# A two-layer transformer on one core: the loop over iterations 2 to 14 written out, waits on constants

## What is computed

```python
x = layernorm(x + L0_attn(x))      # rmsnorm, q/k/v, softmax(q k / 8) v, output projection, bias
x = layernorm(x + L0_ffn(x))       # shared expert + sum over 8 experts, weighted by the top-2 router gates
x = layernorm(x + L1_attn(x))      # per token: 16 heads of 8, scores between heads of the same token
x = layernorm(x + L1_ffn(x))       # sum over 8 experts, weighted by the top-2 router gates
```

## Time and profile before

| | |
|---|---|
| median of 3 runs | 1562.2 us (1561.91 to 1562.41) |
| the profiled execution | 1567.07 us, span 1565.3 us |
| TensorE matmul / weight load, busy | 1421.9 us (91%) / 1249.4 us (80%) |
| VectorE, busy | 985.5 us (63%) |
| ScalarE, busy | 860.9 us (55%) |
| GpSimd, busy | 514.5 us (33%) |
| mean granted TensorE clock | 0.976 |
| start of iteration 2 / 3 / 6 / 14 / 15 (ScalarE's table load for the exponentials) | 176.84 / 269.00 / 545.4 / 1282.6 / 1374.73 us |

### The profile page before, as it was taken

How to read it: one execution, slowest core, us unless ns; L and a number is a source line. 1 busy time by engine, 2 the same in 40 slices (tenths; PEclk the granted TensorE clock), 3 DMA queues, 4 the chain that set the end, 5 groups by cost and what they waited for, 6 DMA issues and landing times.

```text
span 1565.3 us, 34497 instructions
## 1 busy us (share of the span) xinstructions
PE 1421.9 (91%) x12096; PEld 1249.4 (80%) x12096; DVE 985.5 (63%) x2534; ACT 860.9 (55%) x2361; POOL 514.5 (33%) x415
## 2 busy tenths in 40 slices
PE   6897999999999999999999999999999999998847
PEld 5675888888888888878888888888888887887747
DVE  4456576675757667575666757667575766757482
ACT  5564655656465564647556464655646465463403
POOL 3206061340605134060522506043250614315040
PEclk9898999999999999999999999999999999998978
DMA  7000000000000000000000000000000000000000
GB/s 239 4 2 1 5 2 8 0 7 0 0 7 0 7 0 7 0 0 7 0 7 0 7 0 0 7 0 7 0 1 5 0 7 0 3 1 1 4 1 7
DMA packets 14088, 13.78 MB, mean 9 GB/s; under 512 B 1625, under 2 KB 12770, under 8 KB 13794
## 3 DMA queue, kind: packets, MB, share of 16 engines
q1 hardware_dynamic: 14050, 13.27, 2.6%
HBM read 11.17 MB, written 2.10 MB: 8 GB/s over the span
## 4 chain that ended last, share of the span: by engine, by line
issue 62%; POOL 17%; POOLq 14%; PE 4%; DVE 1%; ACT 1%; DMA 0%; DVEq 0%; SPq 0%
POOLq L329 8%; POOL hid L466 6%; POOL hid L471 6%; POOLq L473 5%; POOL std_inv L427 2%; PE bank_F L1101 1%; POOL up_lo L436 1%; POOL x L488 1%; POOL x_plus L450 1%; POOL rms_inv L443 1%; PE bank_S L983 0%; DMA b_out<-in_b_out 0%; ACT probs L544 0%; DVE hid L743 0%; DVE hid L761 0%
## 5 line engine op out<-in xcount | busy, mean ns | idle before, releaser
L1101 PE MATMUL bank_F<-down,hid 128*128 128x128 f32 x3072 | 374.9, 278 | 34.6 <-DVE x L731 34.0
L1101 PEld LDWEIGHTS bank_F<-down,hid 128*128 128x128 f32 x3072 | 359.4, 193 | 46.3 <-DVE x L731 38.1
L544 ACT ACTIVATE probs<-bank_S,neg_max 128x256 f32<-128x256 f32 x512 | 235.5, 475 | 179.0 <-DVE neg_max L652 178.9
L652 DVE TENSOR_REDUCE neg_max<-bank_S 128x2 f32<-128x512 f32 x256 | 164.6, 684 | 83.5 <-PE bank_S L983 80.2
L471 POOL TENSOR_TENSOR hid<-hid,qkv 128x1024 f32<-128x1024 f32 x62 | 177.1, 2857 | 47.1 <-ACT hid L560 47.1
L731 DVE SCALAR_TENSOR_TENSOR x<-bank_F,gates,x 128x128 f32<-128x128 f32 x512 | 155.2, 345 | 31.6 <-PE bank_F L1101 21.4
L523 ACT ACTIVATE probsT<-bank_T 128x512 f32<-128x512 f32 x256 | 139.6, 605 | 44.1 <-PE bank_T L1012 44.0
L426 POOL TENSOR_TENSOR var_eps<-mv,ln_eps 128x2 f32<-128x2 f32 x64 | 12.5, 195 | 428.5 <-DVE mv L690 428.5
L441 POOL TENSOR_TENSOR mean_sq<-sum_sq,one_over_d 128x2 f32<-128x2 f32 x16 | 3.1, 194 | 455.1 <-ACT h_row L518 455.1
L1012 PE MATMUL bank_T<-ident,probs 128*128 128x128 f32 x1024 | 138.4, 279 | 0.1
L459 POOL TENSOR_TENSOR hid<-qkv 128x1024 f32<-128x1024 f32 x47 | 112.2, 2386 | 66.6 <-ACT qkv L523 66.6
(11 more groups left out here) (167 smaller groups left out, 3259.1 us busy)
## 6 DMA issues: line engine op xcount, KB each, us to landing
x_row<-in_x SPq DMA_DIRECT2D x16, 128.0 KB, 2.1
down<-in_w SPq DMA_DIRECT2D x1, 2048.0 KB, 14.0
out<-x SPq DMA_DIRECT2D x16, 128.0 KB, 1.8
hid<-in_w SPq DMA_DIRECT2D x1, 1536.0 KB, 7.8
hid<-in_rw SPq DMA_DIRECT2D x1, 1024.0 KB, 6.6
hid<-in_wv SPq DMA_DIRECT2D x1, 512.0 KB, 3.8
hid<-in_wq SPq DMA_DIRECT2D x1, 512.0 KB, 4.7
hid<-in_wk SPq DMA_DIRECT2D x1, 512.0 KB, 5.6
```

The lines of the kernel that those rows point to most:

```text
L544: ins = sc.activation(probs[:, h // 2 % 2, h % 2, t, :], unit.bank(f"S{h}")[:, t * S:(t + 1) * S], ACT.Exp, bias=neg_max[:, h, t:t + 1], a ...
L652: ve.tensor_reduce(neg_max[:, h, :], v.bank(f"S{h}")[:, :].rearrange("p (t k) -> p t k", t=NT), AX.X, ALU.max, negate=True).then_inc(max_r ...
L1101: ins = te.matmul(bank[:, (j * NT + t) * P:(j * NT + t + 1) * P], hid[:, e, k, tokens(t)], down[:, e, k, :], start=k == 0, stop=k == m - 1)
```

## The change

`run` no longer emits a loop. Each engine's program is the body of all 18 iterations one behind the other, `step` is the constant 0 in all of them, and `it` runs on, so every wait's number is a constant. FIRST and LAST go. Nothing else is touched; line numbers behind L47 fall by one and behind `run` by five.

```diff
-FIRST, LAST = 2, ROWS - 2
...
             if before:
                 before(Before(banks))
-            for it in range(FIRST):
-                body(Iteration(it, 0, banks))
-            with eng.Fori(0, LAST - FIRST + 1) as step:
-                body(Iteration(FIRST, step, banks))
-            for it in range(LAST + 1, ROWS + 2):
+            for it in range(ROWS + 2):
                 body(Iteration(it, 0, banks))
```

## The result

The changed kernel has a median of 1566.72 us over 18 runs (1564.81 to 1568.88), the kernel before, run beside it, 1563.43 (1561.16 to 1566.88, 18 runs). Three of the 18 times of the kernel before are those behind the 1562.2 us that the forecast starts from; the other 15 have a median of 1564.17. The ratio is 1.0015, 95% interval 1.0008 to 1.0022. The medians lie 3.3 us apart and the interval says 1.3 to 3.4 us more, where the forecast was 1.2 us less. One execution of the kernel before in the third comparison took 7720.15 us and counts in no ratio.

The account below looks back on a forecast made before the run. TensorE's matmuls set the pace, 1421.9 us of the 1565.3 us span. Register work saved, -3.5 us, plus VectorE's stops, +2.3, gave -1.2 us, from 1562.2 to 1561.0 us; range 1559.1 to 1563.5.

Parts of the forecast that it names:

- from the profile to the time: Whole kernel: profiled execution forecast at 1565.9 us, timed median taken 4.9 us below it, giving 1561.0.
- Loop, net -1.2 us: Iterations 2 to 14: register work saved, -3.5 us, plus VectorE's stops at instruction blocks, +2.3 us.
- The new scores at an iteration's start: TensorE's idle time ahead of L983 falls from 0.65 to 0.51 us, saving 0.14 us an iteration.
- VectorE's terms: Register arithmetic ahead of VectorE's waits: L778 saves 0.08 us, L794 0.08, L809 0.04; L800 costs 0.07, each iteration.
- Back edge, 0: The loop's compare and branch, taken 12 times: removing it saves 0, as queued work or waits cover it.
- TensorE's blocks, 0: Fetching TensorE's written-out code in every iteration costs TensorE nothing, as iteration 2 lasts as long as iteration 14.
- 26 x 0.36 / 4 = 2.3: VectorE's stops at instruction blocks: two an iteration of 0.36 us, a quarter reaching TensorE, costing 2.3 us.
- rival 2: VectorE's stops between last heads and x1T become the bound, GpSimd's products adding delay: slower, up to 1571.4 us; chance 0.13.
- Rival 3: TensorE's clock falls after longer idle time in some iterations; if every time, 18 us more, 1580 us; chance 0.03.
- Rival 1: VectorE's stops all fall into slack, so the whole 3.5 us saving stays: 1558.7 us; chance 0.25.
- What would show it: Profile signs: L983 idle near 0.5 us, some 26 VectorE gaps, iterations 91.9 to 92.4 us; wrong if clock leaves 1.00.
- Three things change, 13 times each: Iterations 2 to 14: back edge, register arithmetic ahead of waits and place of the code, taken as the whole change.

Follow-up runs that it names:

- the third comparison: The unchanged changed kernel timed again beside the kernel before: 1563.58 us against 1565.64, ratio 0.9988.
- the shifted end: The changed kernel with 25 drains added at the start of VectorE's program of iteration 15: 1564.25 us, ratio 0.999.
- VectorE alone and its drains: The kernel before with only VectorE's program written out, plus 23 drains in iteration 2 and 15 in iterations 3 to 15: 1559.57 us, ratio 0.9957.
- the one with 23 drains: The changed kernel plus VectorE drains, 23 in iteration 2 and 15 in iterations 3 to 15: 1557.59 us, ratio 0.9949; again on another chip 1560.66, 0.9963.

## Why the prediction was wrong where it was

It forecast 1561.0 us, in a range of 1559.1 to 1563.5, and no change that can be told. Measured were 1566.72 us. Its last range, 1556.8 to 1567.0, takes in two rivals and just holds that. By their medians the three comparisons give +3.3, +0.5 and -2.1 us, mean +0.6; the first, beyond its own interval, went the other way.

Two steps failed. The first is from the profile to the time: "The timed runs have a median of 1562.2, 4.9 below it; the same difference gives 1561.0". The changed kernel's profiled execution took 1564.93 us, 1.0 below the 1565.9 forecast for it, but its timed runs have a median 1.8 *above* that, not 4.9 below. The 1562.2 came from three runs. In the later comparisons the kernel before itself has 1565.56 to 1565.91, outside the forecast's range. Of the miss of 5.7 us, 1.2 are this base and 1.2 the net saving that the timed runs don't show; the other 3.3, the rise against the kernel run beside it, stay open, since every profile of the changed kernel has a shorter loop. The second is the sum itself: its first term is 0, its VectorE terms were 2.5 times as large, its stops dearer, and TensorE's clock, left out of the sum, costs 1.4 us in some executions. That they add up to the -1.2 forecast, in the first profile, is luck.

- **Loop, net -1.2 us: the value measured in the first profile, by other terms.** There it is -4.2 + 3.0, where the forecast had -3.5 + 2.3. In the others the sum was 1197.50, 1198.26 (with the shifted end) and 1197.45, so the mean over four is -0.3 against the kernels with a loop (1197.73 to 1197.89).
- **"The new scores at an iteration's start ... saves 0.14": this term failed.** It is 1.8 of the 3.5 us. With TensorE's program alone written out, the idle time at L983 fell by the 0.14 us and the iteration stayed as long: 0.13 us less up to mid-iteration, 0.13 more behind it. That TensorE loses it waiting for VectorE is argued, not shown.
- **VectorE's terms, 0.13 together, measured 0.33.** L778, L794 and L800 are as I took them. At L743 and the second L761 the gap shrinks by 0.08 each, which I missed though the trace of before had their 0.17 of "issue", and at L809 by 0.08 (0.15 to 0.07) instead of 0.04: 0.08 x 5 - 0.07 = 0.33. This account adds up, but no run takes the places one by one: L743 also lasts 3.33 us instead of 3.25, and the same 0.08 goes at an L800 22 us into the iteration and at two L778 behind L809.
- **Back edge, 0, and TensorE's blocks, 0: right in the loop.** TensorE alone and all but VectorE last as long as the loop. The Trainium skill (Runtime: NRT & Kernel Launch, "Instruction fetch mechanics") has crossings mostly hidden: the 73 crossings of TensorE agree, VectorE's 0.35 to 0.42 us do not. It has a fetch at a taken branch only where the target isn't held. The prediction read that as a cost at every back edge; no back edge showed a fetch or a cost, which doesn't contradict the page.
- **"26 x 0.36 / 4 = 2.3": right count and share, too small a sum.** Some 24 stops, six on the path. Five cost 0.19 to 0.39 and together 1.6; one cost 1.23. A stop's price isn't its length: at L789 the mechanism that I kept for rival 2, VectorE falling behind a GpSimd product, triples it. I had it as a case of its own with 0.13, when a creeping stop meets that place once in any case. With a stop at that place in every iteration the kernel took 9.1 us more than the kernel before beside it, as much as rival 2's dearest case (1571.4, 9.2 us more).
- **Rival 3 was put as all or nothing, and as just out of reach.** By the weight loads of the earlier trace rows the idle time would be 1.99 + 0.49 = 2.48 us, "just short" of the 2.53 ahead of a fall. It was 2.32 in iteration 12 of the second profile, and the clock fell. It fell in one iteration, the twelfth, in four of six profiles whose VectorE code is unshifted and written out, at 1.4 us, and in none of the other eight profiles. An estimate for the sum is 4/6 x 1.4, about 1 us.
- **Rival 1, all stops in slack, had to be made.** Its 3.5 us became 4.3 and 4.7 in the loop once the stops were placed.
- **What would show it: right in part.** There is no "issue" ahead of L773, 0.51 at L978, undisturbed iterations last 91.8 where I said about 91.9, and disturbed ones up to 92.2 where I said 92.4. Iteration 10, at 93.05, is outside it. And one sign of being wrong that I named, the clock leaving 1.00 between 165 and 1430 us, came at 1162 us in the changed kernel's second and third profiles, though not in its first.
- **What I left out: "Three things change, 13 times each" takes iterations 2 to 14 for the whole change.** Time less span is 1.80 us for the kernel before and 1.93 for the changed one (means of a comparison's runs), so 0.13 lies outside the span. It is 1.97 with all but TensorE written out, 1.79 with TensorE alone and 1.78 with VectorE alone and its drains, so it comes with the programs of ScalarE, GpSimd or SyncE. And iterations 15 to 17 have other stops than before. The first works against the change, the second may; they may explain part of the first comparison, not its 3.3 us. The rest is open: only profiled executions can be looked into, and two of the same kernel (the one with 23 drains) differ by 1.8 us up to iteration 2 and by 2.0 from iteration 15 on.

## What to carry to other kernels

Here, writing out a loop to save register work paid only on the engine whose operations follow each other behind drains and whose chain the others wait for. In such a case count every place that shows the same "issue" (0.17 us here) on that engine, and no gap on an engine that waits for it. Then look where the instruction blocks end. If the engine stops there, an iteration of a whole number of blocks, padded where it waits anyway, keeps the stops at one harmless place: here 15 cheap drains turned a change of nothing into 4.9 to 8.3 us less than before, of which 4.3 to 4.7 us are shown to be the loop's. And before a forecast in absolute time, take more than three runs of the kernel before: here its medians lay between 1562.2 and 1565.91.

## What was not expected of the hardware

- VectorE stops for 0.35 to 0.42 us each 128 instructions, each time with a block of 8 KB on queue 14 (23 blocks, 0.19 MB, with its program alone written out). TensorE, with blocks of 16 KB on queue 8 (1.20 MB in 73), does not show a stop.
- VectorE's 128x256 subtraction (L761) takes 0.43 us ahead of GpSimd's product and 1.35 if it starts beside one, so 0.4 us of delay becomes 1.2.
- The same instructions, with 1.90 or 1.92 us of idle time at the same place, kept 2.4 GHz once and fell to 1.2 GHz for 3.4 us another time. With 1.73 us or less at that place the loop never fell.
- Three comparisons of the same pair of kernels gave 1.0015, 1.0005 and 0.9988, each with an interval of 0.0007 to 0.001 to either side; the last two ran on different chips. Such an interval holds for its comparison, not for the kernels.
